# Dividing the attention outputs at the end of each step, and writing a two-pass loop out, in a fused scan + local-attention + feed-forward kernel

## What is computed

```python
h = shift_token(x)                     # half of the channels from the token before
q, k, v = split(h @ wqkv)              # 8 heads of 64
q, k = l2norm(q) * qs, l2norm(k) * ksc
q, k = rotary_xpos(q, k)               # cos/sin tables
o = local_attention(q, k, v)           # windows of 64, this window and the one before, softmax
x = x + o @ wo
h = shift_token(x)
h = (h - mean(h)) / sqrt(var(h) + 1e-5) * lg + lb
a, g = split(h @ w1 + b1)
x = x + (a * gelu(g)) @ w2 + b2
```

## Time and profile before

| what | value |
|---|---|
| median of 3 runs | 435.87 us (433.83 to 436.12) |
| span of the profiled execution, first to last instruction | 431.7 us (the profile gives no other time of its own) |
| busy PE / DVE / POOL / ACT | 351.5 / 321.6 / 301.1 / 280.8 us |
| busy PEld | 287.5 us |
| mean granted TensorE clock | 0.941 |
| chain that ended last, by engine | PE 37%, DVE 23%, POOL 19%, issue 11%, ACT 7% |

### The profile page before, as it was taken

The page is one execution under the profiler, slowest core; times in us unless marked ns, Lnnn a source line. Parts: engine busy times, 40 slices in busy tenths (PEclk is TensorE's granted clock), DMA queues, the critical chain, the costliest instruction groups (busy, mean ns, idle before and its releaser), DMA issues.

```text
span 431.7 us, 11030 instructions
## 1 busy us (share of the span) xinstructions
PE 351.5 (81%) x3832; PEld 287.5 (67%) x3832; DVE 321.6 (74%) x751; ACT 280.8 (65%) x844; POOL 301.1 (70%) x247
## 2 busy tenths in 40 slices
PE   1573055899999899999999999999999989988781
PEld 1352034677778687778777887788778867766561
DVE  6889964787689767966796788688869877954653
ACT  3552263688678677867786788678777868764430
POOL 2200419899999889988998699869887988780222
PEclk9996557999999999999999999999999999998966
DMA  7700042412142125112511342043204220220110
GB/s 262 225 0 0 13 125 60 110 27 50 46 118 56 32 55 141 30 30 64 133 32 33 105 94 51 15 121 76 62 3 117 65 53 2 57 57 2 24 49 25
DMA packets 42373, 28.29 MB, mean 66 GB/s; under 512 B 21668, under 2 KB 36566, under 8 KB 42326
## 3 DMA queue, kind: packets, MB, share of 16 engines
q1 hardware_dynamic: 42325, 27.68, 24.4%
HBM read 13.51 MB, written 3.15 MB: 39 GB/s over the span
## 4 chain that ended last, share of the span: by engine, by line
PE 37%; DVE 23%; POOL 19%; issue 11%; ACT 7%; DMA 1%; SPq 1%; POOLq 1%; DVEq 0%; ACTq 0%
POOL rn L507 7%; PE bank L726 5%; POOL rot L552 4%; PE bank L771 4%; DVE rot_sin L1153 4%; PE upper L708 3%; DVE rot_cos L1153 3%; POOL rot L541 3%; ACT probs L902 3%; PE bank L650 2%; PE bank L763 2%; DVE normed L1052 2%; PE upper L659 2%; PE bank L590 2%; DVE neg_max L1201 2%
## 5 line engine op out<-in xcount | busy, mean ns | idle before, releaser
L902 ACT ACTIVATE probs<-upper,neg_max 128x128 f32<-128x128 f32 x256 | 90.4, 369 | 48.5 <-DVE neg_max L1201 48.4
L507 POOL TENSOR_TENSOR rn<-floored,minus_half 128x16 f32<-128x16 f32 x32 | 93.8, 2930 | 2.7
L541 POOL TENSOR_TENSOR rot<-rot_cos,rot_sin 128x512 f32<-128x512 f32 x32 | 40.9, 1277 | 44.3 <-issue 23.6
L1201 DVE TENSOR_REDUCE neg_max<-upper 128x4 f32<-128x512 f32 x64 | 43.1, 684 | 27.5 <-PE upper L708 27.4
L552 POOL TENSOR_TENSOR rot<-rot,rn 128x1024 f32<-128x1024 f32 x32 | 60.9, 1903 | 2.5
L902 ACT ACTIVATION_READ_ACCUMULATOR probs<-upper,neg_max 128x1 f32 x256 | 53.0, 207 | 0.0
L590 PE MATMUL bank<-wqkv_hi,act_t_hi 128*128 128x512 f32 x96 | 43.3, 452 | 7.9 <-DVE act_t_lo L1140 2.8
L1153 DVE TENSOR_TENSOR rot_cos<-bank,tab 128x512 f32<-128x512 f32 x64 | 43.6, 681 | 2.0 <-PE bank L594 1.9
L1153 DVE TENSOR_TENSOR rot_sin<-bank,tab 128x512 f32<-128x512 f32 x64 | 43.4, 679 | 0.0
L542 POOL TENSOR_TENSOR rot<-rot_cos,rot_sin 128x512 f32<-128x512 f32 x32 | 40.9, 1279 | 0.0
L1160 DVE TENSOR_REDUCE ss<-sq 128x16 f32<-128x1024 f32 x32 | 38.7, 1209 | 2.4 <-ACT sq L944 2.3
(11 more groups left out here) (140 smaller groups left out, 863.7 us busy)
## 6 DMA issues: line engine op xcount, KB each, us to landing
v_mid<-v_tok SPq DMA_DIRECT2D x64, 128.0 KB, 2.3
tab_raw<-tables SPq DMA_DIRECT2D x8, 512.0 KB, 3.4
h_tok<-group_in SPq DMA_DIRECT2D x14, 128.0 KB, 3.5
x_res<-group_in SPq DMA_DIRECT2D x28, 64.0 KB, 1.8
wqkv_raw<-wqkv SPq DMA_DIRECT2D x2, 768.0 KB, 6.8
x_in<-x SPq DMA_DIRECT2D x4, 256.0 KB, 3.6
head_scale<-head_scales SPq DMA_DIRECT2D x8, 128.0 KB, 4.0
group_in<-normed SPq DMA_DIRECT2D x4, 256.0 KB
```

The costliest lines, as they stand in the source:

```text
L507: pool.tensor_tensor(rn[:, 0:2 * HEADS], floored[:, 0:2 * HEADS], minus_half[:, :], ALU.pow).then_inc(rn_ready, 1)
L541: pool.tensor_tensor(rot[cur.par][:, :, 0:32], rot_cos[:, :, 0:32], rot_sin[:, :, 32:64], ALU.add).then_inc(rot_added, 1)
L902: last = act.activation(probs[:, h, :], s_bank[half][:, (h % 4) * P:(h % 4 + 1) * P], ACT.Exp, bias=neg_max[a.par][:, h:h + 1], accum_out= ...
L1201: dve.tensor_reduce(neg_max[a.par][:, 4 * half:4 * half + 4], src, AX.X, ALU.max, negate=True).then_inc(max_ready, 1)
```

## The change

Three things change, all in the order of instructions; no operation of the computation is added or left out.

1. On DVE, `invert_sums` and `divide_o` of `mid` stand at the end of every step (they stood so in step 2 alone), and are gone from between the two halves of the row maxima.
2. The statistics of h2 move from the end of step 1 to step 2, behind the row maxima and ahead of `rotate`. The statistics of y, the layer's output, which the last normalisation needs, move from the end of step 3 to step 0 of the next pass, behind the division and ahead of `split_inputs`.
3. `passes` calls `body` with plain numbers for every G. The hardware loop is gone, and with it register arithmetic and the semaphore counts of `settle`.

```diff
-                    if mid.valid and j != 3:
-                        row_max(mid, 0)
-                    if done.valid and j != 3:
-                        invert_sums(done)
-                    if done.valid and j != 3:
-                        divide_o(done)
-                    if mid.valid and j != 3:
-                        row_max(mid, 1)
+                    for half in range(2):
+                        if mid.valid and j != 3:
+                            row_max(mid, half)
+                    if ffn:
+                        dve.wait_ge(h2_in, 64 * G)
+                        variances(h2, h2_var)
                     if cur.valid:
                         rotate(cur)
...
                     if cur.valid:
                         sum_squares(cur)
-                    if norm:
-                        dve.wait_ge(h2_in, 64 * G)
-                        variances(h2, h2_var)
-                    if final:
-                        variances(y, y_var, GT)
-                    if j == 0 and not (number and not 0 <= G < LAST - 1):
-                        split_inputs(G + 1)
                     if ffn:
                         split_h2(G - 1)
+
+                    if mid.valid:
+                        invert_sums(mid)
+                        divide_o(mid)
+                    if j == 0 and G > GROUPS + 1:
+                        variances(y, y_var, GT)
+                    if j == 0 and 0 <= G < LAST - 1:
+                        split_inputs(G + 1)
                     if j == 2:
-
-                        if mid.valid:
-                            invert_sums(mid)
-                            divide_o(mid)
                         for half in range(2):
                             if prev.valid:
                                 row_max(prev, half)
...
-            body(-1, 0)
-            body(0, 0)
-            for layer in range(DEPTH - 1):
-                G0, G1 = GROUPS * layer + 1, GROUPS * (layer + 1) - 1
-                if steps:
-                    steps.enter()
-                with eng.Fori(G0, G1) as G:
...
-            body(LAST - 1, DEPTH - 1, 2)
+            for G in range(-1, LAST - 1):
+                body(G)
+            body(LAST - 1, 2)
             ending()
```

More of the change, by code:

```diff
@@ L224, in sandwich_kernel, with __init__ @@
         dve_chain = sem("dve_chain")
-        settled = {e.name: sem(f"settled_{e.name}") for e in (mybir.EngineType.SP, mybir.EngineType.DVE, mybir.EngineType.Pool, mybir.EngineType.PE)}
         block = ctx.enter_context(nc.Block())
         def need(eng, s, value):
[L231 to L240, removed]
+            if value > 0:
+                eng.wait_ge(s, value)
         class At:
-            def __init__(self, G, j, back, layer):
+            def __init__(self, G, j, back):
                 n = j + 3 - back
@@ L299, in link @@
                 self.catch_up()
[L301 to L309, removed]
         def low_pieces(l):
@@ L417, in _ @@
             sp.dma_start(x_res[:, :, :], normed[:, 0:GT, :]).then_inc(x_res_first, 16)
-            with sp.Fori(1, GROUPS - 1) as g:
-                need(sp, xf_ready, g + 1)
+            for g in range(1, GROUPS - 1):
+                sp.wait_ge(xf_ready, g + 1)
                 store_mixed(g)
@@ L578, in ending @@
                     add_input(g)
-            passes(pool, body, ending)
+            passes(body, ending)
         W_IN = 16 * DEPTH * 12
@@ L787, in body @@
                 for j in range(count):
-                    cur, prev, mid, done, after = (At(G, j, back, layer) for back in range(5))
-                    ffn = j == 2 and not (number and G < 1)
+                    cur, prev, mid, done, after = (At(G, j, back) for back in range(5))
+                    ffn = j == 2 and G >= 1
                     if cur.valid:
@@ L925, in gelus, with body @@
                                    bias=b1_sb[l][0:cn, 3 + c:4 + c]).then_inc(gelu_done, 1)
-            def body(G, layer, count=GT):
-                number = isinstance(G, int)
+            def body(G, count=GT):
                 for j in range(count):
-                    cur, prev, mid, done = (At(G, j, back, layer) for back in range(4))
+                    cur, prev, mid, done = (At(G, j, back) for back in range(4))
                     if mid.valid:
@@ L1225, in place_early @@
             def place_early(G):
-                if not (isinstance(G, int) and G >= LAST - 1):
+                if not (G >= LAST - 1):
                     dve.wait_ge(xa_ready, GT * G + 2)
@@ L1340, in ending @@
                 normalise_out(GROUPS - 1)
-            passes(dve, body, ending, steps)
+            passes(body, ending)
 def kernel(L0_attn_x, L0_attn_W_hg, L0_attn_W_out, L0_ffn_wqkv, L0_ffn_q_scale, L0_ffn_k_scale, L0_ffn_wo,
```

151 lines of the change are left out of this document (61 added, 90 removed).

## The result

The changed kernel took **427.4 us** (median of 6 runs, 426.74 to 428.87), the kernel before beside it 433.75 (6 runs): ratio 0.9845, 95% interval 0.9816 to 0.9873, which is 5.5 to 8.0 us. Of the 4.6 us between 432.0 and 427.4, 2.1 lie in the kernel before: the three runs shown ahead of the prediction, median 435.87, were on the high side. The other 2.45 lie in the change.

A forecast was written before the change was run, and what follows sets the result against it. It took POOL's additions of rotated products, in step 1 waiting for DVE's late rotation, to bound a pass. Savings of 2.2 + 1.7 + 0.8 less 0.8 lost made 3.9 us off 435.87, giving 432.0 us, range 429.6 to 435.6.

The forecast's parts named there:

- the division's 0.83 us: Step 1: the division between the halves of the row maxima holds up all that follows, the rotation included, by 0.83 us.
- POOL's idle time in step 1: POOL's wait at 259.47 for the late rotation on DVE: 0.64 us, forecast to go entirely.
- Loop: Removing the hardware loop from the passes was to save 0.8 us (0.6 to 1.2).
- Ramp: Before the first feed-forward, POOL's four waits for a rotation were to shrink, saving 1.7 us (0.8 to 2.4).
- Four passes: G = 2 to 5: h2's normalisation comes 0.55 us earlier in each pass, 2.2 us together (0.8 to 2.6).
- In step 0 POOL is the limit already, which gives nothing: Step 0 of a pass: POOL itself sets the pace, so an earlier rotation saves nothing there.
- Normalisation starts at 269.04 at the latest: h2's normalisation on DVE, 269.50 before, was to gain 0.46 us at least and 0.64 at best.
- G = 6: Statistics of y delay the input split, the earlier rotation offsets it: nothing gained or lost (0.5 lost to 0.1 gained).
- Statistics of y in G = 7: Standing ahead of the row maxima, for which ACT waits, they were to lose 0.8 us (0.3 to 1.1).
- The next bound takes it: Rival: PE's value products or ScalarE's squares hold h2's transposes, each pass gains only 0.21 us; 434.8 us, chance 0.12.
- No engine does less work, so nothing moves: Rival: DVE and POOL do the same operations, so the time stays at 435.9 us; chance 0.10.
- The wait at the end of the step is exposed: Rival: at the ends of steps 3, 0 and 1 DVE's wait for value products delays others; 439.4 us, chance 0.06.

The follow-up runs named there:

- e1: Changed kernel with DVE's old order back (division between the row-maxima halves, statistics at their old places), passes still written out, no settle counts: 431.25 us, ratio 0.9955.
- e2: Changed kernel with the settle counts of DVE, POOL and PE put back, loop still gone: 428.95 us, ratio 0.9911.
- e3: Changed kernel with the statistics of h2 and y back at the ends of steps 1 and 3, ahead of the division there: 426.32 us, ratio 0.9837.
- e5: Changed kernel run once more, unaltered: 427.86 us, ratio 0.9862.
- e4: Changed kernel with the statistics of y ahead of the division in step 0 instead of behind it: 427.12 us, ratio 0.9866.
- e6: The same kernel as e4, run a second time: 427.75 us, ratio 0.9862.
- e9: Changed kernel with POOL's inverse deviations of h2 ahead of the copy of k_t in step 1: 426.52 us, ratio 0.9820.
- e10: e4 with PE repeating harmless products at its waits in the last 50 us, same output: 423.50 us, ratio 0.9758.

## Why the prediction was wrong in size

The direction and the main mechanism were right: the division's 0.83 us left the path in front of the rotation, POOL's idle time in step 1 went, and the rest followed. By parts, forecast and measured:

- **Loop, 0.8 us; measured 1.6** (e1). "The loop" was priced from the longest pass, 42.61, which stays 0.39 longer than G = 4 without any loop, beside POOL's weight split. What made up for it, and more, was a term I had at nothing: the settle counts, 1.1 us (e2), 0.1 to 0.2 in every pass, written out or not. The loop itself is left with some 0.5, a difference of two runs and not tried by itself. The Trainium skill, page "Runtime: NRT & Kernel Launch", section "Instruction fetch mechanics", says that a taken branch out of the fetched window stalls its engine, and the prediction drew from it that the removal would be worth more than the rows' price. By e1 and e2 it was worth less than the 0.8; no run here shows a stall of this kind by itself.
- **Ramp, 1.7; measured 1.68** (e1 to e3). The step-by-step count of the idle times held: at the four rotations POOL is 0.87, 0.86, 1.17 and 1.66 us earlier in e3 than in e1, where I had 0.83, 0.83, 1.32 and 1.66. Three of the four idle times are gone; the second, 0.28 before, is not printed in the changed kernel's trace, 0.24 in e5 and 0.27 in e3.
- **Four passes, 2.2; measured 3.2** (e1 to e3). Two steps failed. "In step 0 POOL is the limit already, which gives nothing": it waited 0.19 us there, unprinted. And "Normalisation starts at 269.04 at the latest": that made VectorE the limit, from statistics taken at 1.63 us, and brought the forecast down from POOL's 0.64 to 0.55. They take 1.19, and the normalisation simply followed POOL. Their new place did not matter (e3), so neither the cost I gave it nor a benefit was there. What a pass gained was POOL's waits, 0.19 plus 0.62 us.
- **G = 6, nothing; measured 0.23** (e1 to e3): POOL's first step is 8.56 us in e1 and 8.38 in e3 here too, so it waited unprinted.
- **Statistics of y in G = 7, 0.8 lost; measured 0.64**, in the row maxima (e4). The rest of the 1.35 us by which the profiled tail is longer is put down to the granted clock. It falls at the same place in two runs of the changed kernel (e5) and at different places in e4 and e6, and with it one kernel's tail moves by 3.1 us.

Together 1.6 + 1.7 + 3.2 + 0.2 - 0.6 = 6.1 us, beside the 6.35 of the medians (5.5 to 8.0); what the clock does to the tail is not in this sum.

The rivals: "The next bound takes it" did not cut this change, but it is where the next one ends: after it PE's transposes come 31.65 us behind the sum of y in G = 4 and 5 whether POOL is early or not (e9). "No engine does less work, so nothing moves" fell: PE and DVE are busier than before, POOL as busy within 0.2 us, and the time is 1.5% shorter; here waits had to be read, not occupancy. "The wait at the end of the step is exposed" fell: 0.44 to 0.48 us of waiting stand behind the division in steps 3, 0 and 1 of the regular passes.

## What to carry to other kernels

An engine that shows no idle time may still wait: compare the length of its step with the sum of its instructions, and with the same step elsewhere, before calling it the limit. A semaphore instruction that does no work is still an instruction on its engine's path; count it in every pass. Where a few long waits of TensorE stand close together, profiled runs of one kernel can differ by some 3 us with the granted clock (e4, e6); filling these waits with harmless products kept the clock up and took some 4 us off the median (e10).

## What the runs showed of the hardware

- **Counts.** Some 0.2 us a pass for increments of a semaphore that nobody waits for, and about 0.1 us in one place: the gap between the two parts of the statistics, 0.03 us without (changed), 0.14 with a count (e2).
- **The granted clock.** Behind the same waits (1.26 and 0.74 us) it fell to the lower level in e6 and not in e4, where it fell later; the tails differ by 3.1 us; with the waits filled (e10) it did not fall until TensorE's work was over. What decides between e4 and e6 stays open.
- **VectorE and GpSimd.** The split of h2 (both inputs in SBUF) took 0.69, 0.93 or 1.06 us, as GpSimd's addition had 0.09 (e9), 0.37 (changed) or 0.51 us (before) left to run; GpSimd's table product beside it took 1.18 to 1.23 us, and 0.71 to 0.74 in the other steps. The Trainium skill, page "SBUF — State Buffer", section "Who interferes with whom", says that a VectorE instruction with two SBUF inputs contends with a GpSimd instruction that reads SBUF, that the port pair they share is an exclusive lock, and that the order of issue decides who is blocked. The rows agree with a block: with 0.37 and 0.51 us of the addition left the split is 0.24 and 0.37 us longer than in e9, some 0.13 less than what was left both times. That was read from the traces, not tried by itself.
